# Splitting 192 rows as 128 and 64 in six stages, and pairing the units of two attentions

## The reference, cut to what matters

```
h = concat(patches(x), words(x_txt))                       # 16 x 102 x 192
h += attention0(layernorm(h)); h += slot_ffn(layernorm(h))
h += L1(layernorm(h)):  x += ssm(ln(x)) ; x += attn1(ln(x)) ; x += mlp1(ln(x))
h += experts1(layernorm(h))
h += L2(layernorm(h)): softmax attention, 12 heads of 64  ; h += mlp2(layernorm(h))
h += L3(layernorm(h)): (q k^T / sqrt(d) * decay) v        ; h += experts3(layernorm(h))
```

## Time and profile before

| | |
|---|---|
| median of three executions | 1702.41 us |
| profiled execution: span of the engines | 1698.1 us |
| the rest of an execution, median less span | 4.3 us |
| TensorE busy | 1444.5 us, 85% of the span |
| VectorE, ScalarE, GpSimd busy | 683.9, 662.5, 384.9 us |
| inner projection and ssm of L1 | 594 to 667 us |
| attention 1, mlp 1 | 667 to 843.5 us, 845 to 917.6 us |
| attention 2, mlp 2, attention 3 | 1092 to 1350, 1350 to 1421, 1421 to 1474.5 us |

### The profile page before, as it was taken

One profiled execution on the slowest core, in us unless ns is written; L12 is line 12 of the kernel. 1 busy time (PEld: TensorE's weight loads), 2 busy tenths in 40 slices (PEclk: granted clock), 3 DMA queues, 4 the chain that ended last, 5 costly groups with the idle time before them and its releaser, 6 DMA issues.

```text
span 1698.1 us, 31669 instructions
## 1 busy us (share of the span) xinstructions
PE 1444.5 (85%) x10300; PEld 1049.9 (62%) x10300; DVE 683.9 (40%) x2124; ACT 662.5 (39%) x2237; POOL 384.9 (23%) x464
## 2 busy tenths in 40 slices
PE   5899986796756778888899899699999999989994
PEld 3666664632212345666678799466765776789994
DVE  5557766511101376444423622433542423551113
ACT  1667663410000233777842122153663632213331
POOL 5212222300000122222200266220220200123441
PEclk8899996587778688999998899799999999889997
DMA  8434341679998400000003366200000200126553
GB/s 219 133 83 129 82 115 28 227 242 333 311 314 249 147 1 1 1 0 0 0 0 100 107 203 197 81 1 1 0 0 0 93 37 0 30 84 199 181 175 103
DMA packets 94439, 178.73 MB, mean 105 GB/s; under 512 B 35578, under 2 KB 54168, under 8 KB 92704
## 3 DMA queue, kind: packets, MB, share of 16 engines
q1 hardware_dynamic: 80144, 130.65, 26.1%
q10 hardware_dynamic: 7056, 30.67, 5.6%
q0 software_dynamic: 7136, 16.10, 3.1%
HBM read 150.39 MB, written 26.99 MB: 104 GB/s over the span
## 4 chain that ended last, share of the span: by engine, by line
PE 58%; issue 12%; DVE 12%; DMA 8%; ACT 6%; SPq 3%; POOL 1%; DVEq 0%; ACTq 0%; POOLq 0%
PE bank L1819 15%; DMA WM<-in_fc 7%; PE bank L2339 6%; PE bank L2325 4%; PE bank L1910 4%; PE bank L1922 3%; PE bank L1939 3%; PE bank L2329 3%; PE bank L1949 3%; PE bank L2000 2%; PE bank L1885 2%; PE bank L1992 2%; ACT ON L1604 2%; SPq L226 2%; PE bank L2256 1%
## 5 line engine op out<-in xcount | busy, mean ns | idle before, releaser
L1819 PE MATMUL bank<-XT,AREA 96*128 96x408 f32 (+1 forms) x640 | 239.1, 532 | 33.9 <-ACT XT L1558 16.6
L1819 PEld LDWEIGHTS bank<-XT,AREA 96*128 96x128 f32 (+1 forms) x640 | 122.1, 196 | 139.8 <-issue 99.8
L1910 PE MATMUL bank<-KZ,QT 128*102 128x102 f32 x1152 | 140.8, 262 | 9.0 <-ACT PB L1604 5.7
L664 POOL TENSOR_TENSOR PB<-PB,RCU 102x306 f32<-102x306 f32 x96 | 69.2, 720 | 318.5 <-DVE RCU L923 318.4
L648 POOL TENSOR_TENSOR RS<-VE,expo 102x4 f32<-102x4 f32 (+1 forms) x53 | 53.0, 1001 | 387.2 <-DVE VE L863 329.8
L1910 PEld LDWEIGHTS bank<-KZ,QT 128*102 128x102 f32 x1152 | 122.4, 174 | 27.2 <-issue 18.1
L2339 PE MATMUL bank<-WM,KZ 128*128 x660 | 118.2, 327 | 0.0
L2339 PEld LDWEIGHTS bank<-WM,KZ 128*128 128x128 f32 x660 | 105.7, 190 | 0.4
L1585 ACT ACTIVATE KZ<-bank,AREA 128x128 f32<-128x128 f32 x198 | 54.6, 374 | 121.8 <-PE bank L2329 121.8
L1922 PE MATMUL bank<-AREA,OT 128*102 128x192 f32 x384 | 88.9, 345 | 11.3 <-DVE SLOTS L1276 5.3
L1939 PE MATMUL bank<-PT,V 102*32 102x102 f32 (+1 forms) x1152 | 85.9, 270 | 14.5 <-DVE OT L933 12.3
(11 more groups left out here) (335 smaller groups left out, 2777.5 us busy)
## 6 DMA issues: line engine op xcount, KB each, us to landing
AREA<-in_fc SPq DMA_DIRECT2D x10, 1536.0 KB, 26.1
SLOTS<-in_m3w SPq DMA_DIRECT2D x33, 384.0 KB
WM<-in_fc ACTq DMA_DIRECT2D x5, 2304.0 KB, 19.5
WM<-in_fc SPq DMA_DIRECT2D x6, 1536.0 KB, 27.9
AREA<-in_fc ACTq DMA_DIRECT2D x4, 2304.0 KB, 20.6
SLOTS<-in_m1w SPq DMA_DIRECT2D x33, 256.0 KB
AREA<-pos_scratch SPq DMA_DIRECT2D x16, 459.0 KB
pos_scratch<-AREA SPq DMA_DIRECT2D x8, 913.5 KB
```

Of the source, the lines that this page charges most:

```text
L664: pool.tensor_tensor(p, p, scale, ALU.mult).then_inc(sem["probs_ready"], 1)
L1819: last = pe.matmul(dst, lhsT, rhs, start=n == 0, stop=n == len(pieces) - 1)
L1910: last = pe.matmul(psum[k][0:T, cols(j)], QT[:, tile, cols(bb)], KALL[:, unit % per_tile * (HEADS // per_tile) + tile, cols(bb)], start=Tr ...
```

## The change

1. **128 and 64 rows.** In six stages `xt_wide` turns features 0 to 127 into one bank and features 64 to 191 into another. ScalarE copies the first whole; of the second it copies rows 64 to 127 (features 128 to 191) twice, to rows 0 to 63 and 64 to 127 of `XT2`. Two outputs are made together (`split`, `columns`, `value_rows`): a product of 128 rows for each, then one of 64 rows for each, on the upper and the lower half of TensorE's rows, into two banks. TensorE waits for the first copy ahead of the whole products and for the other two ahead of the half ones. The weights' last 64 rows are loaded to both halves of the partitions, in more and smaller loads.
2. **Keys once.** Queries and keys are stored unpadded, 128 rows in a copy (`QT`, `KT`), over four banks in place of two. GpSimd's two clearings of `KZ` and the waits on them are gone.
3. **Paired attention** (attention 1 and 2; attention 0 keeps the old order). The scores of units s and s+1 are made together on different row groups (32 rows each in attention 1, 64 in attention 2), into two of four banks; the values' products of two units follow one another into one bank; probabilities of even units are turned into one bank and copied by ScalarE, those of odd units into another and copied by VectorE (`odd_turns`); there are four buffers for them (`PTS`), and values run six steps behind in place of five.

The core of the diff:

```diff
+            def split(outs, whole, part):
+                for n, dst in enumerate(outs):
+                    last = pe.matmul(dst, *whole(n), start=n < 2, stop=False)
+                    say_taken(last)
+                while behind:
+                    moved(behind.pop())
+                return [pe.matmul(dst, *part(n), start=False, stop=n >= len(outs) - 2) for n, dst in enumerate(outs)]
...
+                def turn(n):
+                    pe.wait_ge(sem["probs_ready"], at.take("probs_ready"))
+                    if n % 2:
+                        k = TBANKS[1]
+                        if n == 1:
+                            pe.wait_ge(sem[f"bank_free{k}"], at.now(f"bank_full{k}") + 1)
+                        else:
+                            turned(n - 2)
+                    else:
+                        k, p = claim(TBANKS[:1])
+                    for j in range(HPU):
+                        last = pe.transpose(psum[k][0:T, cols(j)], PB[n % 4][:, j, :], ident[0:T, 0:T])
...
+                for s in range(STEPS):
+                    if 0 <= s - 3 < UNITS:
+                        turn(s - 3)
...
+                    if s < UNITS and s % 2 == 0:
+                        scores(s)
+                    if 0 <= s - 6 < UNITS and s % 2 == 0:
+                        values(s - 6)
...
+            def odd_turns(n):
+                dve.wait_ge(sem["turn_ready"], at.take("turn_ready"))
+                src = psum[TBANKS[1]][0:T, 0:TU].rearrange("p (h t) -> p h t", h=HPU)
+                give(dve.tensor_copy(PTS[n % 4][:, 0:HPU, :], src), "turn_taken")
+                dve.wait_ge(sem["turn_taken"], at.now("turn_taken"))
...
                     if 0 <= s - 1 < UNITS:
                         inverse_sums(s - 1)
+                    if not pos and 0 <= s - 4 < UNITS and s % 2:
+                        odd_turns(s - 4)
...
-                for j in range(3):
-                    k = at.bank(XBANKS)
-                    src = full(k)[:, 0:TG]
-                    for u in range(UPB):
-                        rows = slice(32 * u, 32 * u + 32)
-                        last = activation(KALL[rows, 3 * u + j, :], src[rows], ACT.Identity,
-                                          bias=bqk1[rows, 3 + j:4 + j])
-                    free(last, k)
+                    free(activation(KT[:, j, :], full(k)[:, 0:TG], ACT.Identity, bias=bqk1[:, 3 + j:4 + j]), k)
...
-            pool.memset(KZ[:], 0.0).then_inc(sem["halves_cleared"], at.one("halves_cleared"))
-            pool.wait_ge(sem["halves_cleared"], at.now("halves_cleared"))
```

More of the change, by code:

```diff
@@ L790, in _ @@
             expert_rows(1)
[L791 to L796, removed]
             powers(1)
@@ L943, in attention, with values_alternate @@
                         between(s)
+            def values_alternate(bias):
+                v5 = by_head(16)
+                for first in range(2):
+                    k = at.bank(OBANKS)
+                    o = full(k)
+                    for n, bb in enumerate((first, first + 2)):
+                        last = tt(v5[:, bb * HEADS:(bb + 1) * HEADS, 0:16],
+                                  o[0:T, n * D:(n + 1) * D].rearrange("p (h d) -> p h d", d=16),
+                                  bias.rearrange("p (h d) -> p h d", d=16), ALU.add)
+                    free(last, k)
             def values(v, dv, bias):
@@ L1870, in pairs, with mlp @@
                 return out
-            def mlp(tiles, w1, x, w2):
-                tokens = []
-                for m in range(tiles):
-                    k, p = claim(FBANKS)
-                    last = product(p[:, 0:TG], [(w1[:, part, m * 128:(m + 1) * 128], x(part)) for part in range(2)])
-                    tokens.append(filled(last, k))
+            def mlp(w1, half, w2):
+                tokens = {}
+                for m in range(FT // 2):
+                    tokens[m], tokens[m + 3] = columns(w1, half, m * 128, (m + 3) * 128, m * 128, FBANKS)
                 for first in range(0, GB, 2):
@@ L2364, in _ @@
             pe.wait_ge(sem["w2_loaded"], 16 * W2_LOADS)
-            pe.wait_ge(sem["halves_cleared"], at.take("halves_cleared", 2))
             with at.loop(pe, NG) as g:
-                xt()
+                xt_wide()
                 qk = []
-                for w in (wq2, wk2):
-                    for p6 in range(6):
-                        k, p = claim(XBANKS)
-                        qk.append(filled(product(p[:, 0:TG], two(w, p6 * 128, (p6 + 1) * 128)), k))
+                for w, half in ((wq2, wq2h), (wk2, wk2h)):
+                    for p3 in range(3):
+                        qk.extend(columns(w, half, p3 * 128, (p3 + 3) * 128, p3 * 128, FBANKS))
@@ L2382, in _ @@
+                    v_moved.extend(filled(ins, k) for ins, (k, p) in zip(last, two_banks))
+                moved(*qk[-4:])
+                paired_attention(2, 64, wo2, v_moved[-2:])
             with at.loop(pe, NG) as g:
-                xt()
-                mlp(FT, wi2, lambda part: XT[:, part, :], wu2)
+                xt_wide()
+                mlp(wi2, wi2h, wu2)
             with at.loop(pe, NG) as g:
-                xt()
+                xt_wide()
                 qk = []
-                for dst in range(4):
-                    k, p = claim(XBANKS)
-                    qk.append(filled(product(p[0:KD, 0:TG], two(wqkv3, dst * KD, (dst + 1) * KD)), k))
@@ L2391, in _ @@
-                v_moved = pairs(lambda bb: token_rows(XT, bb, wqkv3, 2 * D, 3 * D))
-                moved(*qk[-2:])
+                for a in range(2):
+                    qk.extend(columns(wqkv3, wqk3h, a * D, a * D + KD, a * KD, FBANKS, KD))
+                v_moved = value_rows(wqkv3, wv3h, 2 * D)
+                moved(*qk)
                 k, p = claim(SBANKS)
```

296 lines of the change are left out of this document (212 added, 84 removed).

## The result

The changed kernel took 1795.56 us (median of four executions, 1790.73 to 1801.39), the kernel before 1701.45; the ratio is 1.0572, 95% interval 1.0533 to 1.061. The kernel is slower, by more than the 53 us forecast: inside the range, and 6 us above the 1725 to 1790 of the likeliest case. The profiled execution has a span of 1792.9 us, 94.8 more than before. From the page of the changed kernel: span, busy times, and the granted clock in 40 slices.

A forecast was written before the change was run, and what follows sets the result against it. TensorE was taken to bound the six stages. From 1702.4 us, 68 saved at the heads, 67 added by the closed loop and 53 by the clock gave 1754.4, stated as 1755; range 1690 to 1825.

The forecast's parts named there:

- the likeliest case: Whole kernel: head savings, closed loop and partly lowered clock together give 1755 us (1725 to 1790); chance 0.45.
- The bound: Six stages are bound by TensorE; in attention 1 it is busy 37.6 of 43.3 us a group, clock 1.00.
- The closed loop: Paired attentions 1 and 2: one pair in flight, waiting through VectorE's odd copy; 3.9 us a pair, +67 us.
- The clock: Attentions 1 and 2: TensorE's waits lower its granted clock, 44% of the time at 1.2 GHz; +53 us.
- The heads: Stage heads, with clearing and loads: split products, fewer key copies and shorter waits save 68 us in sum.
- Turned tokens, keys, clearing, loads: Per group 0.6 or 0.4 us saved on tokens, 1.9 on attention 1's keys; once, clearing saves 4.0, loads cost 1.
- The clock holding at 1702: Rival: the attentions keep full clock, so heads and loops cancel; 1702 us, give or take 10; chance 0.18.
- the short loop: Rival: the paired attention's loop takes 3.4 us at full clock, giving 1678 us; chance 0.10.
- the low clock throughout: Rival: the clock is low through all of both attentions, +120 us, giving 1822 us; chance 0.22.
- the halves that gain nothing: Rival: half products gain nothing in their new place, 46 us on top of the likeliest, 1801 us; chance 0.03.

The follow-up runs named there:

- e1: The changed kernel with the old attention put back (unpaired order, padded keys and their clearing): 1673.33 us, ratio 0.985 to the kernel before.
- e5: The changed kernel with a pair's scores issued ahead of their step's turns, so two pairs can be in flight: 1711.98 us, ratio 1.0032.
- e2: The changed kernel with VectorE's copy of odd turned probabilities moved ahead of its step's minima and reciprocal: 1743.0 us, ratio 1.0252.
- e4: The changed kernel with six unused identity products on TensorE ahead of each odd turn, where it waited: 1749.92 us, ratio 1.0295.
- e3: The changed kernel with attention 2's values' outputs over four banks in place of two: 1774.66 us, ratio 1.0424.
- e10: As e8, but a set begins on halves where the set before ended on halves: 1646.26 us, ratio 0.9636 to the kernel before.
- e7: As e5, plus attention 2's values over four banks and VectorE's odd copies ahead of minima and reciprocal: 1695.84 us, ratio 0.9965.
- e8: The changed kernel with the old unpaired attention and padded keys, and attention 2's values over four banks: 1658.14 us, ratio 0.9719.
- e11: As e8, but GpSimd clears the keys only after VectorE's first normalisation of attention 1: 1655.26 us, ratio 0.9724 to the kernel before.

## Why the prediction was right, point by point

- **The bound.** Right: where TensorE lost its cover, the time was lost; where it was given back (e1, e5), the time came back.
- **The closed loop.** Right, in place and mechanism: the chain is in the rows step by step, and taking one link out (e2, 4.67 to 3.73 us a loop, 53 us of time) or putting a second pair in flight (e5, 84 us) shortens it. At full clock it is 3.86 us against 3.9 forecast. Two links were off by 0.2 us and cancel: scores to minima is 0.89 us also for twelve half products, and turn to scores 0.40, not 0.23.
- **The clock.** Right that it falls, mis-sized in part: 44% of the attentions' time at 1.2 GHz was forecast, for the parts behind the heads. The rows there were granted 0.53 to 0.59 in attention 1 and 0.69 to 0.75 in attention 2, which are 82 to 94% and 50 to 62%; over whole groups 0.62 to 0.64 and 0.84 to 0.85 (0.78 in attention 2's first). So the share was too small. The price was too high: a loop without a projection piece grew from 3.86 to 4.67 us, 0.8 and not 1.1. The two errors offset each other, and that loop and clock together are 127 us against 120 is in part luck. e4 shows that it is the waiting: with TensorE at work there, the clock was 0.94 to 0.98 in attention 2 and 0.84 to 0.93 in attention 1.
- **The heads.** This is the step that failed in size: 68 us saved were forecast, and 38 came (the rows of the table from the head of attention 1 to the ssm stage). The largest term is attention 2's head, forecast at 20.8 saved, measured at 1.4 lost: I priced the values' sets by TensorE's products alone and passed over that both banks of a set now end together, with no third one to go on in. Three waits of 1.3 us in each of four groups are 16 us, and e3 gives 16 us of attention 2 back. The rest is the change between whole and half products, 0.2 us each where I paid 0.1: in 92 pairs and sets outside the ssm stage that is some 18 us (an estimate from these rows), and e10, which drops about half of the changes, gives 12 us. Together these are 34 of 30, a rough sum, and the ssm stage with clearing and loads gave 2 us more than forecast. The prediction's 0.12 us was a gap between records, and its 0.353 us a product a mean with the ends of the row in it; with 0.342 and 0.2 a pair of outputs saves 0.29 us, not 0.5.
- **Turned tokens, keys, clearing, loads.** Right: attention 1's head 15.6 us of 18, the normalisation at 1.25 us, the loads and padding hidden by 0.6 us where 1 us was charged.
- **The rivals.** The clock holding at 1702 and the short loop didn't come; the low clock throughout (1822) was nearer in attention 1, and the fall ended in the last loops of attention 2 (0.78 to 1.00 in the last one of a group). By its number alone 1795.56 is nearest to the halves that gain nothing (1801); the rows say otherwise: the changes cost more than 0.12 us and took two fifths of the gain of a pair of outputs, not all of it.
- **The miss of 40 us** is then 30 from the heads and 7 from loop and clock; the rest is within the spread of executions.

Why paired attention with two pairs in flight stays above the old order (1695.84 against 1658.14) is only in part known. In the profiles the parts behind the heads are 30 us longer in attention 1 and 12 in attention 2 (e7 against e8), and the other stages give some of it back. In attention 2 the time up to unit 14 goes with the clock, as the two groups of e7 show; the end of a group, at 1.00 in both, is longer too (15.5 to 15.7 us against 14.0 in the first three groups). In attention 1 no group kept its clock without unused products, and no run took away the wait at the start of a group, behind which the clock falls in e5 too. That stays open.

## What to carry to other kernels

Before units are fused so that one engine's work gets shorter, count how many are in flight: a wait on one buffer, in order behind a step that waits for the same unit, can close a loop as long as the whole chain. When two outputs are made to end at the same time, see whether the next two have banks of their own: with two banks TensorE waited 1.3 us a set here, with four not at all. A wait that was put into an inner loop of TensorE's was paid twice here, in the wait and in the clock. And the price of a change is read from start to start of the products around it, not from the gap that their records leave.

## What the runs showed of the hardware

- Changing between products of 128 and of 64 rows took about 0.2 us each way here (four whole ones 1.57 us, four half ones 0.88, with 0.342 us between two whole ones and half of that for half ones). The experts' products of 128 columns in the kernel before cost the same: 0.87 us for twelve half ones, with 0.112 us between two whole ones and half of that for half ones.
- Attention 1 was granted 0.62 to 0.64 at 79% busy, with a wait of TensorE in each loop (1.96 us in the loop from 747.26 to 751.95) and one of 3.26 us ahead of them. The same attention in the old order had 1.00 at 88% busy (e1), and with unused products in the loops' waits 0.84 to 0.93.
- GpSimd's clearing of 4.18 us held up VectorE's normalisation (5.24 us) in e1 as in the kernel before; with the clearing moved behind it (e11) and with none (the changed kernel) it took 1.25 us.
